# A bound for the row numbers of POOL's gathers, held in a register, in a graph layer on one core

## The reference, cut to what matters

```python
h = jnp.maximum(_layernorm(x, axis=-1), 0.0)
# in _L0_gnn_ref(h, edge_index, edge_sh, edge_radial, ...)
x = jax.nn.silu(edge_radial @ W1 + b1)
x = jax.nn.silu(x @ W2 + b2)
tpw = x @ W3 + b3                       # 256 weights for each edge
hs_e, hv_e = hs[src], hv[src]           # rows of h gathered by source
m0 = ALPHA * (einsum('eu,euw->ew', hs_e * sh0[:, None], W00) + INV_SQRT3 * einsum('eui,ei,euw->ew', hv_e, sh1, W110))
m1 = ALPHA * (einsum('eu,ei,euw->ewi', hs_e, sh1, W01) + einsum('eui,euw->ewi', hv_e * sh0[:, None, None], W10))
agg = segment_sum(concatenate([m0, m1]), dst) / sqrt(16)
out = x + h_self + agg
```

## Time and profile before

| | us |
|---|---|
| median of three runs | 614.94 (614.13 to 615.49) |
| the profiled execution | 612.5 |
| its span, first to last instruction or landing | 610.7 |
| gathers on POOL, first start to last start | 3.0 to 237.9 |
| scatters on POOL, first start to last start | 239.2 to 607.1 |

### The profile page before, as it was taken

One profiled execution on the slowest core, in us unless ns is written; L12 is line 12 of the kernel. 1 busy time (PEld: TensorE's weight loads), 2 busy tenths in 40 slices (PEclk: granted clock), 3 DMA queues, 4 the chain that ended last, 5 costly groups with the idle time before them and its releaser, 6 DMA issues.

```text
span 610.7 us, 13180 instructions
## 1 busy us (share of the span) xinstructions
PE 523.4 (86%) x3230; PEld 421.6 (69%) x3255; DVE 464.1 (76%) x1087; ACT 405.4 (66%) x1215; POOL 487.5 (80%) x391
## 2 busy tenths in 40 slices
PE   5777988899879796599998999999999999958780
PEld 4666877688765675577776877777777766745680
DVE  5685777678776877589998699888999989654830
ACT  3433555355556776589998599788998888829330
POOL 6777777777777777888888888888888888888777
PEclk9968999789988759588887688788888788867555
DMA  4754565556631011222222222222222222222222
GB/s 130 194 152 133 182 180 176 152 174 177 186 114 15 14 14 14 10 10 11 11 11 9 11 11 10 10 11 11 11 10 11 10 12 10 10 11 9 9 9 9
DMA packets 54262, 34.40 MB, mean 56 GB/s; under 512 B 37830, under 2 KB 41656, under 8 KB 54200
## 3 DMA queue, kind: packets, MB, share of 16 engines
q0 software_dynamic: 34176, 6.28, 19.0%
q1 hardware_dynamic: 12854, 14.63, 8.2%
q10 hardware_dynamic: 7170, 12.81, 5.7%
HBM read 17.59 MB, written 16.08 MB: 55 GB/s over the span
## 4 chain that ended last, share of the span: by engine, by line
POOL 56%; issue 20%; PE 16%; ACT 3%; DMA 2%; DVE 1%; ACTq 0%; POOLq 0%; DVEq 0%
POOL xg L317 29%; POOL out_dram L330 27%; PE ps L711 6%; PE ps L660 3%; PE ps L714 2%; PE ps L673 2%; DMA out_dram<-sums,idx_i 2%; PE ps L643 2%; ACT dsq L484 2%; PE ps L655 1%; PE ps L638 1%; ACT eq L507 0%; ACT csq L481 0%; DMA src_all<-in_src_dram 0%; DVE msg L1025 0%
## 5 line engine op out<-in xcount | busy, mean ns | idle before, releaser
L330 POOL DMA_INDIRECT out_dram<-sums,idx_i x196 | 307.2, 1567 | 62.6 <-issue 57.7
L317 POOL DMA_INDIRECT xg<-in_x_dram,src_all x186 | 179.4, 964 | 57.7 <-issue 56.5
L711 PE MATMUL ps<-msg,eq 128*128 128x32 f32 (+1 forms) x980 | 142.1, 297 | 14.8 <-DVE carry L983 13.0
L711 PEld LDWEIGHTS ps<-msg,eq 128*128 128x128 f32 x980 | 138.0, 220 | 15.7 <-DVE carry L983 13.4
L1018 DVE TENSOR_REDUCE red<-prod 128x128 f32<-128x1024 f32 x49 | 97.9, 1998 | 0.1
L484 ACT ACTIVATE dsq<-ps,dcol 128x512 f32<-128x512 f32 x196 | 87.5, 546 | 0.2 <-PE ps L673 0.2
L507 ACT ACTIVATE eq<-dsq,onecol 128x384 f32<-128x384 f32 x147 | 73.8, 528 | 0.0
L470 ACT ACTIVATE sums<-ps 128x132 f32<-128x132 f32 x49 | 13.7, 279 | 89.4 <-PE ps L714 73.7
L660 PE MATMUL ps<-w3blk,x 64*128 64x256 f32 x392 | 72.4, 500 | 0.4 <-ACT dsq L484 0.4
L382 ACT ACTIVATE sqT<-ps 128x512 f32<-128x512 f32 (+2 forms) x50 | 29.3, 585 | 60.9 <-PE ps L599 60.5
L660 PEld LDWEIGHTS ps<-w3blk,x 64*128 64x128 f32 x392 | 43.6, 241 | 36.4 <-issue 31.6
(11 more groups left out here) (109 smaller groups left out, 851.0 us busy)
## 6 DMA issues: line engine op xcount, KB each, us to landing
xg<-in_x_dram SPq DMA_DIRECT2D x1192, 0.1 KB
xin<-in_x_dram SPq DMA_DIRECT2D x48, 256.0 KB, 3.1
out_dram<-oc ACTq DMA_DIRECT2D x48, 256.0 KB, 2.6
out_dram<-sums,idx_i POOLq DMA_INDIRECT x196, 3.1
xg<-in_x_dram,src_all POOLq DMA_INDIRECT x186, 2.4
er_all<-in_edge_attr_dram SPq DMA_DIRECT2D x1, 780.0 KB
sh_all<-in_edge_attr_dram SPq DMA_DIRECT2D x1, 390.0 KB
xin<-in_x_dram SPq DMA_DIRECT2D x1, 192.0 KB
```

What stands on the lines that cost most here:

```text
L317: pool.indirect_dma_start(xg[:, t * D:(t + 1) * D], None, x, bass.IndirectOffsetOnAxis(ap=src_all[:, t:t + 1], axis=0)).then_inc(signal, 16)
L330: pool.indirect_dma_start(out, bass.IndirectOffsetOnAxis(ap=idx_i[:, k % NS, a:a + 1], axis=0), sums[:, k % NS, a * DR:a * DR + D], None, ...
L711: m = pe.matmul(psSUM[:, a * DR:a * DR + n], eq[:, k % 2, o:o + P], msg[:, k % 2, b, 0:n], start=(b == a), stop=(not carried and (b == a - ...
```

## The change

A register of POOL is filled once with the number of the last row, 99999, ahead of the gathers' wait for `src_all`. Each of the 186 gathers names this register as the bound of its row numbers and says that a number beyond it is no error, so that such a row would be left out. No row number of this input is beyond it. Before, a gather names no bound, and a bad row would be reported as an error. The 196 scatters, the row DMAs of SP and everything else stay as they are.

```diff
+            last_row = pool.to_reg(N - 1)
+
             def gather(t):
                 signal = gathered[t // GT] if t < GF else gathered_late[int(t >= GF + 30)]
                 pool.indirect_dma_start(xg[:, t * D:(t + 1) * D], None, x,
-                                        bass.IndirectOffsetOnAxis(ap=src_all[:, t:t + 1], axis=0)).then_inc(signal, 16)
+                                        bass.IndirectOffsetOnAxis(ap=src_all[:, t:t + 1], axis=0), bounds_check=last_row,
+                                        oob_is_err=False).then_inc(signal, 16)
```

## The result

The changed kernel takes 618.49 us (median of five runs, 617.4 to 620.35) against 614.39 us (613.92 to 615.49), by these medians 4.1 us more, a third of the 13.0 us that were forecast. The quotient of the two medians is 1.0067; the ratio estimated from all these runs is 1.0083, with a 95% interval of 1.0048 to 1.0117, that is 2.9 to 7.2 us. So it is slower, by some 4 to 5 us. The profiled execution took 620.35 us, the longest of the five, with a span of 618.6 us.

What follows compares the result with a forecast made beforehand. POOL's list of gathers and scatters sets the end, with 2.8 us of slack. 186 gathers at 85 ns more give 15.8 us, less 2.8 is 13.0; 614.94 + 13.0 = 627.9 us, range 613.5 to 690.0.

Steps and rivals of the forecast that it cites:

- a gate: Sum opening unit 14 near the end waits 9.29 us, to 540.10 us, for SP's rows; lateness up to that has no effect.
- 186 d: Shift of POOL's first scatter: 186 gathers times d, the extra time per gather; 15.8 us at 85 ns.
- the price of the bound: Extra POOL time per gather for comparing 128 row numbers: 85 ns, range zero to 601 ns; moderate price given 0.43.
- The cover: POOL's excess waits near the end, before blocks 44 and 46: 2.8 us that vanish and are won back.
- the 2.44 us between profile and median: Median of the runs lies 2.44 us above the profiled execution of 612.5 us; the forecast keeps this distance.
- Unit 12: DVE's use of gathered tiles there has a cover of 77 ns per gather; at 85 ns it would wait 1.1 us.
- unit 13: Its opening sum on DVE already waits 0.26 us for POOL's gathers and moves with POOL.
- unit 14: Its opening sum on DVE stays at 540.1 us, with a wait shorter than 9.29 us.
- A free bound: Rival: the comparison costs a gather nothing, or up to 22 ns; time the same, 614.9 us; chance 0.33.
- The costly way: Rival: rows prepared one by one, a gather costs what a scatter does, 601 ns more; 723.9 us; chance 0.20 from 300 ns.
- My reading of the packets: Queue's 34176 packets as 186 x 32 + 196 x 144: one data packet per engine in gathers, per row in scatters, plus 16.
- The chance of relief for the loads: Rival: lighter gathers cut DVE's 31.9 us waits for chunks of `x` by 3.2 us; 611.7 us; chance 0.04.

Runs made afterwards that it cites:

- before_no_rows: Kernel before without SP's 1192 row DMAs, last ten tiles filled by ten plain loads of other rows; 608.99 us against 612.45, ratio 0.9945.
- fewer_rows: Kernel before with tiles from 120 on split into gathers of 64 and 32 rows, odd tiles with bound and no error; 780.84 us, 324 gathers.
- the five shifts: Five kernels with bounded gathers, the changed kernel among them, whose first scatter starts 6.1 to 18.4 us later than before; slower by 1.9 to 14.9 us.
- before_again: Kernel before, unchanged, profiled a second time; median 613.35 us, ratio 1.0009, profiled execution 614.51 us.
- skip_only: Changed kernel without the bound, gathers only say that a bad row is no error; 612.06 us, ratio 0.9982 to the kernel before.
- half_bound: Kernel before with bound and no error only on the 93 gathers of odd tiles; 615.00 us against 613.12, ratio 1.0033.

## Why the prediction went as it did

**What bounds the kernel** was right. POOL's list of 186 gathers and 196 scatters sets the end, and its time by the sum (605.9 us for the last scatter, some 609.8 us for the execution) was met by `before_no_rows` with 608.99 us. The direction and the mechanism were right as well: more per gather, a later first scatter, a gate that wins part of it back. Of the signs it named, the first scatter came where 239.2 us plus 186 d puts it (249.0 us), the last started 1.0 us later than its rule has it (615.0 against 604.3 + 9.7 = 614.0 us), and the scatters' 1553 ns and the 34176 packets stayed.

**The step that failed is the price of the bound.** I took 85 ns, the distance between two small instructions, because comparing 128 numbers seemed work of that size. It is 52 ns. Of that, about 38 ns come with the instruction whatever its rows (`fewer_rows`), which is much nearer to the register move of 29 ns that I had set aside; what comes with the rows is at most some 16 ns. What POOL does in the 38 ns no run shows. The row was the wrong one in a second way: between gathers such an instruction costs 45 ns, since it goes into the gap. The term is 186 x 0.052 = 9.7 us instead of 15.8.

**The cover was undersized.** I took 2.8 us, from a single profile that was faster (612.5 us) than any of the five timed runs beside it. The distance of the median from the time of POOL's list is the better measure: 612.45 - 608.99 = 3.5 us on one chip, and the five shifts gave 3.5 to 5.7 by the medians, 3.8 to 5.2 by the ratios. I had noted the 2.44 us between profile and median and added them to the result, which assumes that they stay; by `before_again`, a single execution, they are waits of POOL for a later gate, and are used up like the 2.8 us. With both terms put right the sum is 9.7 - 2.8 - 2.4 = 4.5 us, which fits 4.1 (2.9 to 7.2 by the interval).

**The rest, point by point.** The filling of the register was hidden, as set. The gap of 0.305 us did not change. Unit 12 did not wait; unit 13 waits 5.59 us for its gathers instead of 0.26, which I had not sized: DVE comes to it at 244.6 us, and the gathers land later by 9.8 us. `before_no_rows`, without a bound, has a wait of 5.30 us there as well, so nothing shows that it had an effect of its own. The gate's wait did not shrink, as I had said, but was gone altogether, and unit 14 came at 548.74 us. The prediction let the pipeline be late at unit 14 by no more than POOL's shift. It was later by more: DVE was ready for it at 530.8 us before (540.10 less the wait of 9.29), and at 543.2 and 548.7 us in the two profiles of the changed kernel, 12 and 18 us later for 9.8 of shift. For the difference between these two the clock is the likely reason; the rest is open. It cost little, because POOL's own list is what ends last.

**The rivals.** A free bound fell with the 1004 ns; a free flag, which I had not taken apart from the bound, is what `skip_only` showed. The costly way fell too, and its ground with it: the 601 ns are accumulation, and left-out rows take POOL's time and packets like all others. My reading of the packets held, in 23200 and 38592 as well. The chance of relief for the loads found no support in 612.06 against 613.23 us with the flag alone. As to the Trainium skill's statement that descriptor generation is small and the increment shows late (DMA: Bandwidth & Descriptors, "Anatomy of one DMA — SWDGE (gpsimd) path"): for the rows the trace agrees, with 94 ns of POOL's time for 96 rows more. That it would make a bound free was my step, since the page speaks of the number of descriptors and says nothing there on a bound; and on a list that is full even 38 ns per instruction arrive at the end.

## What to carry to other kernels

Where an engine's list is full from start to end, multiply the change per instruction by the count, and then ask how far the kernel's median, not one profiled execution, lies above the time of that list: that distance is the cover, and it is spent once. An unknown option of an instruction should be split into its parts, because here the flag was free and the bound was not. And before moving work to where an engine looks idle, check that it is: one tile given from a gate's engine to the bound one brought 1.6 us, eight rows instead of seven lost 1.8.

## What the runs showed of the hardware

- A gather by row numbers on POOL costs 869 ns with 32 rows, 922 with 64 and 963 with 128, and 0.305 us of gap: almost all of it is by the instruction. It has 32 packets with 32 rows as with 128 (38592 in all in `fewer_rows`).
- A bound adds 38 to 54 ns in four kernels and 66 ns in `half_bound`; with error reporting 13 to 28 ns more. To report no error without a bound changes nothing (965 and 965 ns in one kernel, 954 against 952 between two).
- Rows beyond the bound cost POOL what others cost (1004 ns) and leave the packets at 34176; only their bytes are not moved.
- Accumulation adds some 560 to 680 ns to a scatter of 128 rows (991 ns without, 1553 and up to 1667 with), and a packet for each row.
- A register move of 29 ns, and most of an iota of 143 ns, fit into the 0.305 us gap before an indirect DMA: the iota moved the gathers 45 ns apart, 29 of them by a longer gather.
